# An FFN, RWKV and routing block in another order, with inverses from logarithm and exponential

## The chip, the cores and the metric

One core of a Trainium2 chip runs the whole program. The metric is the device time of one execution in microseconds. The core has five engines with a queue each: TensorE (PE), VectorE (DVE), ScalarE (ACT), GpSimd (POOL) and SyncE (SP). They meet only through semaphores that the program waits on and raises.

## The reference

Two layers over 8 x 256 tokens of 128 channels, all in float32. The change is in the three middle steps:

```python
x = x + attention(layernorm(x))
x = x + ffn(layernorm(x))              # silu(x Wg) * (x Wu), then Wd; hidden 384
x = x + rwkv(layernorm(x))             # time mix, K V R, a scan over time, sigmoid(R) * wkv, Wo
x = x + moe(layernorm(x))              # softmax over 8 experts, top 2, capacity 320

# rwkv, one step in time: a running maximum keeps the exponentials in range
p = max(pp, U + k);  e1 = exp(pp - p);  e2 = exp(U + k - p)
y = (e1 * aa + e2 * v) / (e1 * bb + e2)
p2 = max(pp + w, k); e1b = exp(pp + w - p2); e2b = exp(k - p2)
aa, bb, pp = e1b * aa + e2b * v, e1b * bb + e2b, p2
```

`layernorm` divides by the root of variance plus 1e-5. The routing gives each token its two best experts and its place in each expert's list, which is a count over all tokens before it.

## The kernel before

Three phases stand one after the other: `attention_phase`, `mid_phase` (FFN, RWKV and routing, the only one that the diff touches) and `moe_phase`. The residual `x_res` stays in SBUF.

`mid_phase` works in four chunks of 512 tokens (two sequences of 256). For a chunk, the FFN (suffix f) normalises on ScalarE (`normalize_f`), transposes on TensorE through the bank `xt`, copies back on ScalarE (`copy_f`), makes three gate and three up products of 512 columns (HB is 3), a silu each on ScalarE, their product `h` on VectorE (`hidden`), and `down`. VectorE adds the result to `x_res` and takes mean and variance. The RWKV part (w) normalises, transposes and copies in the same way; `project_k`, `project_v`, `project_r` are two products each (this token and the one before); `running_max` is a scan on VectorE along time, `subtract_max` one more product into the bank of k; `weigh` makes the four exponentials e1b, e2b, e1, e2 on ScalarE (four relus and four Exp); `states` runs the scans aa and bb; `total` makes numerator and denominator; `invert` is VectorE's reciprocal; `finish` multiplies by it and by the gate (sigmoid, on ScalarE); `output` is the product with Wo. The routing part (m) adds, normalises and transposes again, makes logits (`logit`), and on VectorE `shift` (subtract the largest), `choose` (softmax and the two best) and `place` (slot numbers, from TensorE's `count`). GpSimd then writes the chunk's rows to DRAM with eight indirect DMAs.

The order on each engine is written by hand. In slot s the FFN works on chunk s, the RWKV part on chunk s - 1 up to its reciprocal, and `finish`, output and routing on chunk s - 2; `slot_of` of each engine's block lists the calls. There are six slots. A table load (`ACT_TABLE_LOAD`) is put in by the compiler wherever ScalarE goes to a function of another table set; the program doesn't name it. The inverse deviation of the layer norms is made on VectorE: an integer guess and three Newton steps (`rsqrt`, L69 to L77). The banks in PSUM: xt, u, y, d, v, r and two for the gates; logits go to u, the counts and both sums to y.

Of the kernel before, what the change touches and what calls it, by code (L numbers as in the profile page):

```python
# [885 lines left out]
def mid_phase(nc, ffn, wkv, moe, state, x_res, ln_ffn, sem_of, load_next):  # L886
# [6 lines left out]
    with ExitStack() as ctx:  # L893
# [3 lines left out]
        def bank(name):  # L897
# [13 lines left out]
        silu = [sb(f"silu{i}", [P, CW]) for i in range(2)]  # L911
# [23 lines left out]
        ln = normal_tiles(lambda n, s: sb("ln_" + n, s), 2 * TPC)  # L935
        OF_W, OF_M = 0, TPC
# [30 lines left out]
        def _(pool):  # L967
            g = nc.gpsimd
            g.memset(pp[:, :, 0:1], MIN_P).then_inc(consts, 1)
            g.memset(aa[:, :, 0:1], 0.0).then_inc(consts, 1)  # L970
            g.memset(bb[:, :, 0:1], 0.0).then_inc(consts, 1)
# [19 lines left out]
        def _(pe):
# [6 lines left out]

            def transpose_f(c):
                pe.wait_ge(xf_ready, c + 1)  # L1000
                if c > 1:
                    pe.wait_ge(xwT_ready, c - 1)
                transpose(lambda a: xf[:, a, :], tf_done)

            def transpose_w(c):
                pe.wait_ge(xw_ready, c + 1)
                if c > 1:
                    pe.wait_ge(xmT_ready, c - 1)
                elif c < LAST:
                    pe.wait_ge(xfT_ready, c + 2)  # L1010
                transpose(lambda a: xw[:, a, :], tw_done)

            def transpose_m(c):
                pe.wait_ge(xm_ready, c + 1)
                pe.wait_ge(xfT_ready, min(c + 4, CHUNKS))
                if c:
                    pe.wait_ge(xwT_ready, min(c + 2, CHUNKS))
                    pe.wait_ge(xmT_ready, c)
                transpose(lambda a: rows[:, c * TPC + a, 0:P], tm_done)

            def gate_and_up(c, k):
# [674 lines left out]
```

## Time and profile before

| what | value |
|---|---|
| median of 3 runs | 540.08 us (539.99 to 543.14) |
| the profiled execution | 542.5 us, its span 540.5 us |
| mean granted TensorE clock | 0.835 |
| `attention_phase` | 0 to 275.7 us |
| `mid_phase` with its scatters | 275.7 to 460.1 us |
| `moe_phase` | 460.1 to 540.5 us |
| busy in 275.7 to 303.0 us | PE 16.3, DVE 9.6, ACT 9.8 us |
| busy in 303.0 to 329.4 us | PE 18.2, DVE 16.8, ACT 14.9 us |
| busy in 400.7 to 428.6 us | PE 10.8, DVE 21.0, ACT 10.2 us |
| busy in 428.6 to 449.4 us | PE 5.6, DVE 10.7, ACT 3.7 us |

The profile is one execution; the span runs from its first instruction to its last, and 2.0 us lie around it. Times in a timeline count from the span's start. A row gives start, duration, engine, line, operation, output and inputs, and in brackets the idle time before it and what ended it. The granted clock is the share of TensorE's full speed: 1.00 is its 2.4 GHz level, 0.50 its 1.2 GHz level.

### The profile page before, as it was taken

The numbers are of one execution on the slowest core, as the hardware profiler recorded it, in microseconds if no ns is written. First come the engines' busy times: TensorE is split into PE (matmuls) and PEld (weight loads), VectorE is DVE, ScalarE is ACT, GpSimd is POOL, SyncE is SP. The second block draws the span as 40 slices with busy tenths as digits, with TensorE's granted clock in tenths as the row PEclk, the third lists the DMA queues.
The fourth block names the chain that finished last, engine by engine and source line by source line (L and its number), as shares of the span: only waits on it lengthen the run. The fifth ranks groups of instructions, "written<-read, shape, count | busy, mean of one in ns | idle before, by whom it ended". The sixth has DMA issues, their size and how long they took to land. (4 is left out here: it accounts for less than half of the span.)

```text
span 540.5 us, 6922 instructions
## 1 busy us (share of the span) xinstructions
PE 366.8 (68%) x2345; PEld 230.8 (43%) x2345; DVE 289.9 (54%) x706; ACT 235.2 (44%) x399; POOL 179.4 (33%) x342
## 2 busy tenths in 40 slices
PE   2779889898989898787474949478455120489930
PEld 1335454646464655454352434344323110368820
DVE  5646767484848566542634266775777741022224
ACT  1757776374848384431033254653425120163400
POOL 2225473535352647542230000005023135005550
PEclk9879999899999899987778787867767555589985
DMA  9300000000000000000038000001000000413317
GB/s 175 96 1 2 0 2 1 1 0 2 1 1 1 2 0 2 1 1 0 0 68 327 0 0 1 1 1 45 0 11 28 8 9 4 111 57 114 118 38 232
DMA packets 32257, 19.80 MB, mean 37 GB/s; under 512 B 12146, under 2 KB 29955, under 8 KB 31840
## 3 DMA queue, kind: packets, MB, share of 16 engines
q1 hardware_dynamic: 26128, 14.92, 9.8%
q0 software_dynamic: 1920, 2.89, 1.7%
q10 hardware_dynamic: 4176, 1.57, 1.1%
q8 instruction: 18, 0.29, 0.2%
q14 instruction: 15, 0.12, 0.1%
HBM read 12.12 MB, written 8.29 MB: 38 GB/s over the span
## 5 line engine op out<-in xcount | busy, mean ns | idle before, releaser
L537 DVE TENSOR_TENSOR at_attn<-at_sim,at_attn 128x1024 f32<-128x1024 f32 x64 | 75.4, 1219 | 54.7 <-ACT at_attn L414 54.5
L414 ACT ACTIVATE at_attn<-at_sim 128x1024 f32<-128x1024 f32 x64 | 62.2, 1028 | 49.4 <-PE at_sim L234 49.1
L987 POOL DMA_INDIRECT mo_slots<-ro_rows,ro_put x32 | 31.8, 995 | 142.7 <-DVE ro_put L1390 134.2
L251 PE MATMUL at_av<-at_attn,at_v_raw 128*64 128x256 f32 x512 | 64.1, 394 | 11.8 <-DVE at_v_raw L528 11.8
L631 POOL TENSOR_TENSOR at_osq<-at_ob 128x512 f32<-128x512 f32 x32 | 35.9, 1127 | 48.3 <-ACT at_ob L422 47.7
L271 PE MATMUL at_misc<-at_w_out,at_ob 128*128 128x128 f32 x256 | 39.3, 327 | 17.9 <-DVE at_ob L542 17.9
L251 PEld LDWEIGHTS at_av<-at_attn,at_v_raw 128*64 128x64 f32 x512 | 34.5, 139 | 37.4 <-DVE at_v_raw L528 15.0
L271 PEld LDWEIGHTS at_misc<-at_w_out,at_ob 128*128 128x128 f32 x256 | 38.0, 240 | 19.9 <-issue 18.8
L234 PE MATMUL at_sim<-at_q,at_k 32*128 32x256 f32 x512 | 38.7, 401 | 4.0 <-DVE at_attn L537 2.2
L1504 POOL DMA_INDIRECT mo_answers<-mo_ye,mo_to x24 | 22.8, 951 | 41.7 <-DVE mo_ye L1604 36.8
L200 PE MATMUL at_misc<-at_w_v,at_xnT 128*128 128x512 f32 x64 | 34.7, 644 | 0.6 <-ACT at_sq_v L392 0.5
L234 PEld LDWEIGHTS at_sim<-at_q,at_k 32*128 32x128 f32 x512 | 24.0, 184 | 18.0 <-issue 9.3
L422 ACT COPY at_ob<-at_av 128x512 f32<-128x512 f32 x32 | 18.8, 587 | 19.0 <-PE at_av L251 19.0
L1567 ACT ACTIVATE mo_hT<-mo_h,mo_b 128x320 f32<-128x320 f32 x32 | 16.3, 528 | 20.2 <-PE mo_h L1524 20.1
L521 DVE TENSOR_REDUCE at_z<-at_sq_v 128x16 f32<-128x1024 f32 x16 | 19.5, 1218 | 10.1 <-ACT at_sq_v L392 10.1
L1524 PE MATMUL mo_h<-mo_xeT,mo_w 128*128 128x320 f32 (+1 forms) x64 | 22.0, 493 | 3.5 <-ACT mo_hT L1567 2.6
L1533 PE MATMUL mo_y<-mo_w,mo_hT 128*128 128x128 f32 (+1 forms) x192 | 24.4, 281 | 0.0
L391 ACT COPY at_v_raw<-at_misc 128x512 f32<-128x512 f32 x32 | 18.8, 587 | 12.1 <-PE at_misc L200 12.0
L1533 PEld LDWEIGHTS mo_y<-mo_w,mo_hT 128*128 128x128 f32 (+1 forms) x192 | 23.0, 178 | 2.5 <-issue 0.6
L1600 DVE TENSOR_TENSOR mo_ye<-mo_y,mo_b 128x128 f32<-128x128 f32 (+1 forms) x24 | 5.4, 281 | 32.7 <-PE mo_y L1533 23.9
L528 DVE TENSOR_TENSOR at_v_raw<-at_v_raw,at_key_factor 128x1024 f32<-128x1024 f32 x16 | 19.9, 1282 | 5.7 <-POOL at_key_factor L651 5.5
L996 PE MATMUL mi_xt<-ff_ident,ro_rows 128*128 128x128 f32 x16 | 4.5, 433 | 26.8 <-ACT ro_rows L1141 26.8
(208 smaller groups left out, 678.1 us busy)
## 6 DMA issues: line engine op xcount, KB each, us to landing
mo_w<-in_L_ffn_w SPq DMA_DIRECT2D x16, 256.0 KB, 2.9
mo_answers<-mo_zero SPq DMA_DIRECT2D x2, 1024.0 KB, 12.3
mo_got<-mo_answers SPq DMA_DIRECT2D x8, 256.0 KB, 4.7
mo_slots<-mo_empty SPq DMA_DIRECT2D x1, 1440.0 KB, 9.5
mo_xe<-mo_slots SPq DMA_DIRECT2D x5, 256.0 KB, 4.4
x_res<-in_L_attn_tokens SPq DMA_DIRECT2D x4, 256.0 KB, 3.3
out<-x_res ACTq DMA_DIRECT2D x4, 256.0 KB, 2.7
at_w_v<-in_L_attn_Wkv ACTq DMA_DIRECT2D x1, 512.0 KB, 5.7
```

The costliest lines, as they stand in the source:

```text
L200: mm(bank[:, :], xnT[b % 2][:, t * P:(t + 1) * P], w_v[:, half * 512:(half + 1) * 512], start=True, stop=True).then_inc(v_done, 1)
L234: last = mm(sim[h // 2][:, h % 2, j * T:(j + 1) * T], k[b % 2][n % 2][at, n // 2, j * P:(j + 1) * P], q[b % 2][at, n // 2, :], start=True, ...
L251: last = mm(av[e * DV:(e + 1) * DV, half * T:(half + 1) * T], v_raw[b % 2][:, j, h * DV:(h + 1) * DV], attn[(2 * Q + half) % 4][:, e, j, : ...
L271: last = mm(bank[:, t * P:(t + 1) * P], ob[b % 3][:, s, t * P:(t + 1) * P], w_out[:, s, :], start=s == 0, stop=s == PAIRS - 1)
L414: nc.scalar.activation(attn[n % 4][:, :, :, :].rearrange("p e j t -> p e (j t)"), sim[half][:, :, :], ACT.Relu).then_inc(relu_ready, 1)
L528: last = v.tensor_tensor(heads, heads, key_factor[b % 2][:, t, :].unsqueeze(2).to_broadcast([P, HEADS, DV]), ALU.mult)
L537: v.tensor_tensor(r, sim[half][:, :, :], r, ALU.mult).then_inc(attn_ready, 1)
L631: g.tensor_tensor(osq[b % 2][:, 2 * n:2 * n + 2, :], o, o, ALU.mult).then_inc(osq_ready, 1)
L987: g.indirect_dma_start(moe.slots, bass.IndirectOffsetOnAxis(put[k][:, t:t + 1], 0), rows[:, t, :], None, bounds_check=SLOTS - 1, oob_is_er ...
L1504: g.indirect_dma_start(answers, bass.IndirectOffsetOnAxis(to[0:r, 3 * e + n:3 * e + n + 1], 0), ye[e % 2][0:r, n, :], None, bounds_check=2 ...
L1524: mm(h_bank[k][:, 0:CAPACITY], w1[e.par][:, k * P:(k + 1) * P], xeT[:, bass.ds(e.count(CAPACITY), CAPACITY)], start=True, stop=True).then_ ...
L1533: done = mm(y_bank[e.par][0:r, n * P:(n + 1) * P], hT[e.par][:, k, at:at + r], w2[e.par][:, k, :], start=k == 0, stop=k == KB - 1)
```

## The change

Everything is in `mid_phase`.

- **Order.** `slot_of` becomes `period`, for c from -3 to 4: gates and silus of chunk c + 3, ups, `h` and `down` of chunk c + 2, normalising and projections of chunk c + 1, the mixing of chunk c with its inverse, `finish` and output, and the routing of chunk c - 1. There is one gate bank instead of two, three `silu` tiles instead of two, and separate banks for the FFN's and the output's sums (`yf`, `yw`); logits and counts go to `yw`, those of the last chunk to `v`.
- **Inverses.** The reciprocal of the denominator is exp(-ln(den)) on ScalarE, in place on `inv_den`, with one Newton step in `finish`: numerator and denominator are both multiplied by it, q = (den*inv - 2) * num*inv, and -1 in the last product. The inverse deviation is exp(-0.5 ln(var + eps)) (`seeds`) with one Newton step of three VectorE instructions. At the end of each period ScalarE makes an Exp of one column into `spare`.
- **Joint sums.** aa and bb lie in one tile `sums`; e2 and e2*v in one tile `here`; `total` and the first product of `finish` work on both halves at once (1024 columns).
- **Waits.** `normalize_f(0)` comes after the wait for six constants, one of which needs the decay. GpSimd waits for each of the two columns of slot numbers apart.

```diff
@@ banks
-        xt, u_bank, y_bank, d_bank, v_bank, r_bank = (bank(n) for n in ("xt", "u", "y", "d", "v", "r"))
-        g_bank = [bank(f"g{i}") for i in range(2)]
+        xt, g_bank, u_bank, d_bank, v_bank, r_bank, yf_bank, yw_bank = (
+            bank(n) for n in ("xt", "g", "u", "d", "v", "r", "yf", "yw"))
...
@@ TensorE
-            def slot_of(f, x, m):
...
+            def gate_of(c, k):
+                n = HB * c + k
+                pe.wait_ge(xfT_ready, c + 1)
+                if n:
+                    pe.wait_ge(silu_ready, n)
+                mm(g_bank[:, :], ffn.w_gu[:, 0, k * P:(k + 1) * P], xfT[c % 2][:, :], start=True, stop=True).then_inc(gate_done, 1)
...
+            def period(c):
+                gates, hidden, ahead, behind = chunk(c + 3), chunk(c + 2), chunk(c + 1), chunk(c - 1)
+                if chunk(c):
+                    subtract_max(c)
...
+                if behind:
+                    count(c - 1)
+                if gates:
+                    gate_of(c + 3, 1)
+                if hidden:
+                    down(c + 2)
+                if gates:
+                    gate_of(c + 3, 2)
+                if chunk(c) and c < LAST:
+                    output(c)
...
@@ ScalarE
+            def seeds(c):
+
+                first, end = OF_W if chunk(c + 1) else OF_M, OF_M + TPC if chunk(c - 1) else OF_M
+                act.wait_ge(var_ready, c + 2)
+                nc.scalar.activation(ln["var"][:, first:end], ln["mv"][:, first:end, 1], ACT.Ln, bias=eps[:, :]).then_inc(log_var, 1)
+                act.wait_ge(log_var, c + 2)
+                nc.scalar.activation(seed[:, first:end], ln["var"][:, first:end], ACT.Exp, scale=-0.5).then_inc(seed_ready, 1)
+
+            def invert(c):
+
+                act.wait_ge(totals, c + 1)
+                if c:
+                    act.wait_ge(scaled_ready, c)
+                nc.scalar.activation(full(inv_den), total_of[:, 1, :, :], ACT.Ln).then_inc(log_ready, 1)
+                act.wait_ge(log_ready, c + 1)
+                nc.scalar.activation(full(inv_den), full(inv_den), ACT.Exp, scale=-1.0).then_inc(inv_ready, 1)
...
+            def period(c):
+                gates, ahead, behind = chunk(c + 3), chunk(c + 1), chunk(c - 1)
+                if chunk(c):
+                    weigh(c)
+                if ahead or behind:
+                    seeds(c)
+                if ahead:
+                    normalize_w(c + 1)
+                if behind:
+                    normalize_m(c - 1)
+                if ahead:
+                    copy_w(c + 1)
+                if chunk(c):
+                    invert(c)
...
+                if ahead:
+                    gate(c + 1)
+                if gates or ahead:
+                    nc.scalar.activation(spare[:, :], eps[:, :], ACT.Exp)
...
@@ VectorE
+            def inverse_deviations(c):
+
+                first, end = OF_W if chunk(c + 1) else OF_M, OF_M + TPC if chunk(c - 1) else OF_M
+                var, rstd, a, y = ln["mv"][:, first:end, 1], ln["rstd"][:, first:end], ln["a"][:, first:end], seed[:, first:end]
+                dve.wait_ge(seed_ready, c + 2)
+                link(stt(a, var, LN_EPS, y, ALU.add, ALU.mult))
+                link(stt(a, a, -0.5, y, ALU.mult, ALU.mult))
+                link(stt(rstd, a, 1.5, y, ALU.add, ALU.mult))
+                shifts(ln["shift"], ln, first, end, ln_ready)
...
-                link.done(tt(full(t2), full(e2), by_batch(v_bank), ALU.mult))
+                tt(here[:, 0, :, :], e2, by_batch(v_bank), ALU.mult).then_inc(v_used, 1)
                 dve.wait_ge(sums_ready, 2 * c + 2)
-                link.done(tt(full(t3), full(e1), bb[:, :, 0:T], ALU.mult))
-                tt(full(t1), full(e1), aa[:, :, 0:T], ALU.mult).then_inc(v_used, 1)
-                link.wait()
-                tt(full(den), full(t3), full(e2), ALU.add).then_inc(den_ready, 1)
+                link(tt(past[:, :, :, :], sums[:, :, :, 0:T], e1[:, :, :].unsqueeze(1).to_broadcast([P, 2, NB, T]), ALU.mult))
                 dve.wait_ge(v_used, c + 1)
-                tt(full(num), full(t2), full(t1), ALU.add).then_inc(totals, 1)
...
+                tt(total_of[:, :, :, :], past[:, :, :, :], here[:, :, :, :], ALU.add).then_inc(totals, 1)
...
-                link(tt(full(num), full(num), full(inv_den), ALU.mult))
+                tt(scaled[:, :, :, :], total_of[:, :, :, :], inv_den[:, :, :].unsqueeze(1).to_broadcast([P, 2, NB, T]),
+                   ALU.mult).then_inc(scaled_ready, 1)
+                dve.wait_ge(scaled_ready, c + 1)
+                link(stt(full(q), scaled[:, 1, :, :], -2.0, scaled[:, 0, :, :], ALU.add, ALU.mult))
                 dve.wait_ge(gated, c + 1)
...
+                stt(full(rw), full(q), -1.0, by_batch(r_bank), ALU.mult, ALU.mult).then_inc(rw_ready, 1)
...
+            def period(c):
+                behind = chunk(c - 1) and c <= LAST
+                form = chunk(c + 2)
+                if c == 0:
+                    variances(c)
+                if chunk(c):
+                    running_max(c)
+                if c and (chunk(c + 1) or behind):
+                    variances(c)
+                if c == -1:
+                    hidden(c + 2, 0)
+                if chunk(c):
+                    states(c)
+                if chunk(c + 1) or behind:
+                    inverse_deviations(c)
+                if chunk(c):
+                    total(c)
+                if form and c != -1:
+                    hidden(c + 2, 0)
+                if chunk(c):
+                    finish(c)
+                if behind:
+                    shift(c - 1)
+                if c == LAST:
+                    variances(c + 1)
+                    inverse_deviations(c + 1)
...
```

On TensorE, from the start of `mid_phase` (mi_xt transposes, mi_g gates, mi_u ups, mi_y and mi_yf down, mi_d the projection k), before:

```order
L996 MATMUL mi_xt<-ff_ident,mi_xf 128x128 x4
L1026 MATMUL mi_g<-mi_xfT,ff_w_gu 128x512
L1031 MATMUL mi_u<-mi_xfT,ff_w_gu 128x512
L1026 MATMUL mi_g<-mi_xfT,ff_w_gu 128x512
L1031 MATMUL mi_u<-mi_xfT,ff_w_gu 128x512
L1026 MATMUL mi_g<-mi_xfT,ff_w_gu 128x512
L1031 MATMUL mi_u<-mi_xfT,ff_w_gu 128x512
L996 MATMUL mi_xt<-ff_ident,mi_xf 128x128 x4
L1041 MATMUL mi_y<-ff_w_dn,mi_h 128x128 x12
L996 MATMUL mi_xt<-ff_ident,mi_xw 128x128 x4
```

and in the changed program:

```order
L1013 MATMUL mi_xt<-ff_ident,mi_xf 128x128 x4
L1040 MATMUL mi_g<-mi_xfT,ff_w_gu 128x512 x3
L1047 MATMUL mi_u<-mi_xfT,ff_w_gu 128x512 x2
L1013 MATMUL mi_xt<-ff_ident,mi_xf 128x128 x4
L1047 MATMUL mi_u<-mi_xfT,ff_w_gu 128x512
L1040 MATMUL mi_g<-mi_xfT,ff_w_gu 128x512 x2
L1055 MATMUL mi_yf<-ff_w_dn,mi_h 128x128 x12
L1040 MATMUL mi_g<-mi_xfT,ff_w_gu 128x512
L1047 MATMUL mi_u<-mi_xfT,ff_w_gu 128x512
L1013 MATMUL mi_xt<-ff_ident,mi_xw 128x128 x4
```

The three gates of a chunk now stand ahead of its ups, and `down` of chunk 0 comes behind chunk 1's first two gates.

On ScalarE, from the end of `weigh` of chunk 1 (ro_rows and mi_xw are normalised rows of the routing and the RWKV part, mi_xmT and mi_xwT their transposed copies), before:

```order
L1200 ACTIVATE mi_e<-mi_u 128x512 x2
L1165 COPY mi_xfT<-mi_xt 128x512
L1141 ACTIVATE ro_rows<-x_res,mi_ln_shift,mi_ln_rstd 128x128 x4
L1177 COPY mi_xmT<-mi_xt 128x512
L1141 ACTIVATE mi_xw<-x_res,mi_ln_shift,mi_ln_rstd 128x128 x4
L1208 ACTIVATE mi_logits<-mi_logits 128x32
L1171 COPY mi_xwT<-mi_xt 128x2x256
```

and in the changed program:

```order
L1225 ACTIVATE mi_here<-mi_u 128x512
L1231 ACT_TABLE_LOAD
L1231 ACTIVATE mi_ln_var<-mi_ln_mv,mi_eps 128x8
L1233 ACT_TABLE_LOAD
L1233 ACTIVATE mi_seed<-mi_ln_var 128x8
L1166 ACTIVATE mi_xw<-x_res,mi_ln_shift,mi_ln_rstd 128x128 x4
L1166 ACTIVATE ro_rows<-x_res,mi_ln_shift,mi_ln_rstd 128x128 x4
L1196 COPY mi_xwT<-mi_xt 128x2x256
L1240 ACT_TABLE_LOAD
L1240 ACTIVATE mi_inv_den<-mi_total 128x512
L1242 ACT_TABLE_LOAD
L1242 ACTIVATE mi_inv_den<-mi_inv_den 128x512
```

Two logarithms and two exponentials have come in, with a table load ahead of each; the inversion stands behind both normalisings and `copy_w`.

On TensorE, the end of the phase (mi_rw the RWKV result, mi_mask the chosen experts), before:

```order
L1076 MATMUL mi_y<-wk_w_o,mi_rw 128x128 x4
L996 MATMUL mi_xt<-ff_ident,ro_rows 128x128 x4
L1086 MATMUL mi_u<-mo_rw,mi_xmT 128x8 x4
L1096 MATMUL mi_y<-mi_mask,mi_tri 128x32
L1100 MATMUL mi_y<-mi_mask,mi_ones 128x32 x12
```

and in the changed program:

```order
L1102 MATMUL mi_yw<-mo_rw,mi_xmT 128x8 x4
L1091 MATMUL mi_yf<-wk_w_o,mi_rw 128x128 x4
L1110 MATMUL mi_yw<-mi_mask,mi_tri 128x32
L1114 MATMUL mi_yw<-mi_mask,mi_ones 128x32 x8
L1114 MATMUL mi_yw<-mi_mask,mi_ones 128x24
L1114 MATMUL mi_yw<-mi_mask,mi_ones 128x16
L1114 MATMUL mi_yw<-mi_mask,mi_ones 128x8
L1013 MATMUL mi_xt<-ff_ident,ro_rows 128x128 x4
L1102 MATMUL mi_v<-mo_rw,mi_xmT 128x8 x4
```

Output 3 now stands ahead of the count of chunk 2, and the last chunk's transposes behind that count.

## Rows read from the trace of the kernel before

**Rows 1.** Stretches, two middle slots: us, busy of PE, PEld, DVE, ACT, POOL; clock

```profile
329.40:364.80 35.40, 24.50 (x86) 13.82 (x85) 25.01 (x78) 17.87 (x32) 0.00 (x0) 0.78 0.00 1
364.80:400.70 35.90, 22.04 (x78) 12.91 (x78) 24.96 (x79) 13.40 (x24) 7.95 (x8) 0.74 0.05 17
```

**Rows 2.** Waits, 275 to 461 us: total us, times, longest us

```profile
ACT mi_silu L1184 <- PE mi_g L1026: 29.8, 11, 7.2
```

**Rows 3.** Timeline of ScalarE, first relus of `weigh`: start us, us

```profile
310.64 1.24 ACT L1197 ACTIVATE mi_u<-mi_d,mi_decay 128x512 f32<-128x512 f32 x2
...
338.39 1.24 ACT L1197 ACTIVATE mi_u<-mi_d,mi_decay 128x512 f32<-128x512 f32 x2
...
374.25 1.26 ACT L1197 ACTIVATE mi_u<-mi_d,mi_decay 128x512 f32<-128x512 f32 x2
...
404.27 1.26 ACT L1197 ACTIVATE mi_u<-mi_d,mi_decay 128x512 f32<-128x512 f32 x2 [9.72 <-PE mi_d L1058]
```

**Rows 4.** Timelines of VectorE and GpSimd, the last `place` and the last scatter

```profile
447.55 0.19 DVE L1384 TENSOR_SCALAR mi_over<-mi_y 128x32 f32<-128x32 f32 x1 [0.68 <-PE mi_y L1100]
...
449.19 0.17 DVE L1390 CAST ro_put<-mi_top 128x4 uint32<-128x4 f32 x1
...
459.05 0.97 POOL L987 DMA_INDIRECT mo_slots<-ro_rows,ro_put  x1 [0.30 <-issue]
```

**Rows 5.** Timeline of ScalarE, `weigh` of chunk 0 and a small exponential

```profile
311.90 1.28 ACT L1200 ACT_TABLE_LOAD   x1
313.20 0.63 ACT L1200 ACTIVATE mi_e1b<-mi_u 128x512 f32<-128x512 f32 x1
...
315.39 1.14 ACT L1200 ACTIVATE mi_e<-mi_u 128x512 f32<-128x512 f32 x2
...
355.98 0.23 ACT L1208 ACTIVATE mi_logits<-mi_logits 128x32 f32<-128x32 f32 x1 [1.18 <-DVE mi_logits L1356]
```

**Rows 6.** Timeline of ScalarE, `normalize_w` and `copy_w` of chunk 1

```profile
322.05 1.65 ACT L1141 ACTIVATE mi_xw<-x_res,mi_ln_shift,mi_ln_rstd 128x128 f32<-128x128 f32 x4 [5.04 <-DVE mi_ln_shift L1247]
324.90 0.59 ACT L1171 COPY mi_xwT<-mi_xt 128x512 f32<-128x512 f32 x1 [1.21 <-PE mi_xt L996]
```

**Rows 7.** Timeline of VectorE: inverse deviation, sums, reciprocal, end of `choose`

```profile
293.02 0.17 DVE L1290 TENSOR_SCALAR mi_ln_var<-mi_ln_mv 128x4 f32<-128x4 f32 x1
...
295.41 0.16 DVE L1247 SCALAR_TENSOR_TENSOR mi_ln_shift<-mi_ln_mv,mi_ln_rstd 128x4 f32<-128x4 f32 x1
...
321.93 0.68 DVE L1323 TENSOR_TENSOR mi_t<-mi_e,mi_v 128x512 f32<-128x512 f32 x1
...
324.94 3.35 DVE L1334 RECIPROCAL mi_inv_den<-mi_den 128x512 f32<-128x512 f32 x1
...
359.55 0.18 DVE L1377 SCALAR_TENSOR_TENSOR ro_rows<-mi_hot,mo_tokens 128x32 f32<-128x32 f32 x1
```

**Rows 8.** Timeline of TensorE: down, transposes, projections, `subtract_max`

```profile
288.10 2.84 PE L1041 MATMUL mi_y<-ff_w_dn,mi_h 128*128 128x128 f32 x24
...
297.31 1.11 PE L996 MATMUL mi_xt<-ff_ident,mi_xw 128*128 128x128 f32 x4 [6.36 <-ACT mi_xw L1141]
299.19 2.05 PE L1046 MATMUL mi_d<-mi_xwT,wk_w_old_k 128*128 128x512 f32 x2 [0.77 <-ACT mi_xwT L1171]
301.03 1.91 PE L1047 MATMUL mi_d<-mi_xwT,wk_w_k 128*128 128x512 f32 x2
...
309.53 1.02 PE L1046 MATMUL mi_v<-mi_xwT,wk_w_old_v 128*128 128x512 f32 x2
...
366.28 2.08 PE L1058 MATMUL mi_d<-mi_pp,wk_minus 128*128 128x512 f32 x2 [3.13 <-DVE mi_pp L1302]
```

**Rows 9.** Stretches, columns as in rows 1: one low, one high clock

```profile
297.00:303.00 6.00, 4.93 (x9) 2.50 (x10) 0.02 (x1) 0.84 (x2) 0.00 (x0) 0.50 0.00 0
...
331.00:344.00 13.00, 12.73 (x57) 7.70 (x55) 6.81 (x17) 8.81 (x16) 0.00 (x0) 1.00 0.00 1
```

**Rows 10.** The page's part 5: a VectorE product of 1024 columns, in attention

```profile
L537 DVE TENSOR_TENSOR at_attn<-at_sim,at_attn 128x1024 f32<-128x1024 f32 x64 | 75.4, 1219 | 54.7 <-ACT at_attn L414 54.5
```

More of the change, by code:

```diff
@@ L910, in mid_phase @@
         xf, xfT = sb("xf", [P, TPC, P]), [sb(f"xfT{i}", [P, CW]) for i in range(2)]
-        silu = [sb(f"silu{i}", [P, CW]) for i in range(2)]
+        silu = [sb(f"silu{i}", [P, CW]) for i in range(HB)]
         h = sb("h", [P, HB, CW])
@@ L956, in mid_phase, with chunk @@
         block = ctx.enter_context(nc.Block())
-        def chunks(s):
-            return tuple(c if 0 <= c < CHUNKS else None for c in (s, s - 1, s - 2))
+        def chunk(c):
+            return 0 <= c < CHUNKS
+        PERIODS = range(-3, CHUNKS + 1)
         @block.sync
@@ L1131, in _ @@
             pe.wait_ge(ffn.w_ready, 2)
-            transpose_f(0)
-            for s in range(CHUNKS + 2):
-                slot_of(*chunks(s))
+            for c in PERIODS:
+                period(c)
         @block.scalar
@@ L1186, in weigh @@
             def weigh(c):
                 act.wait_ge(d_done, c + 1)
-                if c:
-                    act.wait_ge(sums_ready, 2 * c)
-                    act.wait_ge(totals, c)
-                for pair, exps in enumerate(((e1b, e2b), (e1, e2))):
-                    below, above = ((decay[:, 0:1], decay[:, 1:2]), (cols[:, 1:2], minus_u[:, :]))[pair]
+                for half, exps in enumerate(((full(e1b), full(e2b)), (full(e1), e2))):
+                    below, above = ((decay[:, 0:1], decay[:, 1:2]), (cols[:, 1:2], minus_u[:, :]))[half]
+                    if c and half:
+                        act.wait_ge(totals, c)
+                    elif c:
+                        act.wait_ge(sums_ready, 2 * c)
@@ L1278, in add_mixed, with variances @@
[L1278 to L1295 removed]
+            def variances(c):
+                f, m = c + 1, c - 1
+                if chunk(f):
+                    dve.wait_ge(down_done, f + 1)
+                    add(f, yf_bank, xf_added)
+                if chunk(m):
+                    dve.wait_ge(out_done, m + 1)
+                    add(m, out_bank(m), xw_added)
+                if chunk(f):
+                    dve.wait_ge(xf_added, f + 1)
+                    statistics(f, OF_W)
+                if chunk(m):
+                    dve.wait_ge(xw_added, m + 1)
+                    statistics(m, OF_M)
+                if chunk(f) and f:
+                    dve.wait_ge(xw_ready, f)
+                if chunk(m) and m:
+                    dve.wait_ge(xm_ready, m)
+                link.wait()
+                for a in range(OF_W if chunk(f) else OF_M, OF_M + TPC if chunk(m) else OF_M):
+                    last = v.bn_aggr(ln["mv"][:, a, :], ln["stats"][:, a, :])
+                last.then_inc(var_ready, 1)
@@ L1353, in shift @@
                 dve.wait_ge(logits_done, c + 1)
-                link(tt(full(logits), u_bank[:, 0:TPC * EXPERTS].rearrange("p (t e) -> p t e", e=EXPERTS), each(rb), ALU.add))
+                link(tt(full(logits), route_bank(c)[:, 0:N].rearrange("p (t e) -> p t e", e=EXPERTS), each(rb), ALU.add))
                 link(v.reduce_max(top[:, :], full(logits), AX.X))
@@ L1422, in _ @@
             dve.wait_ge(consts, 6)
-            for s in range(CHUNKS + 2):
-                slot_of(*chunks(s))
+            for c in range(-2, CHUNKS):
+                period(c)
+            shift(LAST)
+            choose(LAST)
+            place(LAST)
 def moe_phase(nc, inputs, state, a, out, x_res, sem_of):
```

282 lines of the change are left out of this document (109 added, 173 removed).

## The prediction

> **What bounds the kernel now.** I read the stretches of the profile first: what the change touches runs from 275.7 us to the last scatter's end at 460.0 [rows 4], 184.3 of the 540.5 us of the span, and no engine fills it. In the two middle slots (329.4 to 400.7 us) VectorE is busy 50.0 of 71.3 us, TensorE 46.5, ScalarE 31.3 [rows 1]. The waits say why: ScalarE alone waits 29.8 us for TensorE's gates, in 11 pieces [rows 2]; TensorE waits 6.4 us for ScalarE's normalised rows at 297.3 and 3.1 for VectorE's scan at 366.3 [rows 8]. It is a ring of three engines in which work passes from one to the next. So it is the length of one way round that counts, and the timeline gives it. I use as its beat the start of the first relu of `weigh`: 310.64, 338.39, 374.25 and 404.27 us [rows 3]. After the last there are 45.1 us to the end of the last `ro_put` cast (449.36) and 10.7 more to the end of the last scatter (460.02) [rows 4].
>
> **The prices** that I take. `weigh`: relus 1.26 us, table load 1.28, then 3.33 from the first exponential to the end of the last (313.20 to 316.53) [rows 5]; so 4.6 without the load. Four normalising activations 1.65 us, a copy of 128x512 0.6 [rows 6]. A chained VectorE step of 4 or 8 columns 0.2 us [rows 7]. The routing choice takes 3.45 us with its wait for the exponential (356.21 to 359.73) [rows 5, 7], `place` 1.8 (447.55 to 449.36) [rows 4]. TensorE: four transposes 1.1 us, or half of it, one product of 512 columns 1.9 us at a pitch of 1.84, or 1.0 [rows 8] (a projection is two: 3.7 or 1.9); the first price of each stands where the granted clock is 0.50 (the 1.2 GHz level), the second where it is 1.00 (2.4 GHz) [rows 9]. TensorE was at the low level after 6.4 and 3.1 us of idling [rows 8].
>
> **What is taken out.** VectorE loses the reciprocal of 3.35 us per chunk [rows 7], and 13 chained steps of the inverse deviation and shifts (293.02 to 295.57, 2.55 us) become 4 (0.8). Its five sums (321.93 to 324.94, a pitch of 0.60 [rows 7]) become one of 512 and two of 1024 columns: the nearest row of 1024 is 1.22 us [rows 10], so 3.0 again. `finish` has 1024, 512 and 512 columns instead of two of 512: 2.6 us for 1.4. The exponentials' load ahead of `weigh` moves to the end of the period, after the gate.
>
> **What is put in.** The trace has no Ln. I price it as the Exp rows of its two sizes, 0.23 us (128x32) and 0.63 (128x512) [rows 5]; an Ln of twice the price would add 0.8 us a period. What weighs more is the order of the change's program: it has a table load ahead of each Ln and one ahead of each Exp that follows it. Every load here takes 1.28 us [rows 5], so the seeds take 1.28 + 0.23 + 1.28 + 0.23 = 3.0 us between `weigh` and the shifts, and the inversion 1.28 + 0.6 + 1.28 + 0.6 = 3.8 us on ScalarE, behind `normalize_w`, `normalize_m` and `copy_w`, where VectorE's 3.35 us lay beside other engines' work and delayed only `place` and the next scan.
>
> The load rows are also where a page can be weighed. The exponential that follows the load starts at 313.20, 0.02 us after its end, and the relu before ended at 311.88, 0.02 us ahead of it [rows 3, 5]: a switch costs 1.3 us in this kernel. The Trainium skill ("ScalarE: Activation LUTs", What ACT_TABLE_LOAD costs) gives 1283 ns too, but adds a drain of 1380 ns, 2.66 us for each switch; with some 21 more switches on the path that would add an estimated 29 us. The trace shows no such drain, and the sum leaves it out.
>
> **The front.** Before, chunk 0 went through gate, up and down in one go, down ending at 290.94, and the first `weigh` began at 310.64 [rows 3, 8]. Now three periods stand ahead of period 0. I walk them with the prices above, from ScalarE's first normalising at 276.7 (some 0.7 us later than before, as it now waits for the decay too): normalised, transposed and copied at 279.75, gate 0 (1.4) ends 281.2; with one gate bank each gate waits for the silu before, so gate 2 ends 285.3; ups 0 and 1, transposes of chunk 1 (after a load of 1.3 and 1.65 of normalising) to 289.8, up 2, gates 1.0 and 1.1, and only then down 0: 293.2 to 296.1, against 290.9. ScalarE's silu of gate 1.2, the spare load, Ln and Exp with their loads put the seeds at 302.2, the normalised chunk at 304.75; transposes (1.1), copy and `project_k` (low level) to 310.4; up, chunk 2's transposes, `project_v`, up, `project_r`, two gates to 318.8; down 1 to 321.5. VectorE's order has chunk 1's variances ahead of the first scan, so scan 0 begins only at 323.7. ScalarE meanwhile: last silu 323.1, load and gate 325.0, load and spare Exp 326.5. First `weigh`: 326.5, which is 15.9 us later.
>
> **The periods,** each from `weigh` (0). Period 0: seeds 7.6, shifts 8.45, normalised 10.15, transposed 11.35, copied 12.0, inversion 15.8, normalising chunk 3 17.45, its transposes and copy 18.85; TensorE: `project_v` 20.0, up, `project_r` 22.6, gate, silu, gate 25.2, down 28.0, gate 28.9; silu 29.5, load and gate 31.4, load and spare 32.9. So 32.9 (before 27.75): 5.15 more. Period 1: shifts 8.45, two normalisings 11.7, copy 12.3, inversion 16.1, `finish` 18.8, `shift` 19.5, an `h` and the routing choice (3.45) 23.6, last `h` 24.3, `place` (1.8) 26.1 beside down 3 (27.2), output 28.1, `subtract_max` 29.1: 29.1 (before 35.86), 6.75 less. Period 2: the same to 18.8, `shift` 19.5, choice 23.3, count and `place` 25.8, scan 27.2, `subtract_max` 29.0 (before 30.02): 1.0 less. The last: one normalising ends 10.15, inversion 14.0, `finish` 16.7, output 3 at the low level 18.85, sum and variances 20.85, seeds 22.65, shifts 23.5; then VectorE does the choice of chunk 2 (27.0), count, `place` 29.4; TensorE's count 2 stands ahead of the transposes of chunk 3 (28.6), copy 29.25, logits 31.15, `shift`, choice 35.6, count, `place` 38.0 (before 45.1): 7.1 less. POOL's scatters come every 1.27 us (0.97 and 0.30 idle [rows 4]): chunk 2's eight run from 29.5 to 39.7, so chunk 3's end at 49.6 (before 55.75), which gives back 1 us.
>
> **Sum:** +15.9 + 5.15 - 6.75 - 1.0 - 6.15 = +7.1 us. The phase after it (80.4 us) is not changed. The profiled execution took 542.5 us, 2.0 around its span of 540.5; the sum makes it 549.6. It was 2.4 above the median of 540.1, so on the median: 547.2 us, 1.3% more.
>
> **Rivals.** *TensorE fast throughout* (24 in 100). The low level costs the walk 0.7 + 0.5 + 1.9 + 0.2 in the front, 0.5 in period 0, 0.6 in period 2 and 1.0 + 0.5 + 0.8 at the end, 6.7 us: 540.5, no change. Against it, waits of 3 us and more remain in every period, and such waits lowered the clock [rows 8, 9].
> *TensorE slow in the front* (18). The gates now pause 0.65 us for each silu, which the trace never shows in a row. If the clock stays at 1.2 GHz to the first scan, some ten products of 512 columns (0.85 each) and a down (2.84) cost 9 to 11 us more: 557 us.
> *VectorE is the bound after all* (10), the other side. Its work falls by 4 x (3.35 - 1.2) + 6 x 1.75 us, 19 in all; were it busy all round, that came off whole and the front's delay would vanish under it: 521 us. It is busy 70% in the middle slots [rows 1], so it decides only where it never waits; it waits for ScalarE's seeds and inverse by the new order.
> *No switch between Ln and Exp* (6), also faster. On the path are 2 loads in the front, 4 in each of periods 0 to 2 and 5 in the last: 19 x 1.28 = 24.3 us, 523 us; below 6 of them left, it is no slower than before. Against it: the order lists all of them. The Trainium skill ("ScalarE: Activation LUTs", Table sets: the hidden batching unit) has this rule, one load for ln and exp in a joint set; no run here shows it.
> The forecast itself has 42.
>
> **How the numbers follow.** The forecast's own range is 543 to 552: the Ln bound (+3), 2 to 4 us of the clock either way. The whole range is 537 to 558: up to the slow front, down past the fast clock; the two cases at 521 and 523 are left out with 16 in 100. A measurement tells about 1% from no change (534.7 to 545.5). Faster takes the cases of 521 and 523 but for 2 in 100, where half of what they take off is given back: 0.14. Same takes those 2, the fast clock's 24 and 4 of the forecast's low edge: 0.30. Slower is the rest: 0.56.
>
> **What would show it.** In the changed profile: the first `weigh` relu near 326 us (310 to 315 would break the front's step); beats of 33, 29 and 29 us after it; a load of 1.28 us before each Ln and each Exp of seeds and inverse, with nothing between but the Ln; the last cast near 455 us and the last scatter near 467, with its eight following chunk 2's without a pause. I am wrong if down 0 ends before 293, or if the inversion ends less than 3 us after `copy_w`.

## The result and the profile after

The changed kernel takes 551.55 us (median of 4 runs, 550.41 to 555.24) against 541.61 us for before beside it (4 runs): a ratio of 1.019, 95% interval 1.012 to 1.026. It is slower, by 9.9 us on the medians; 547.2 was forecast. The profiled execution took 550.4 us, its span 548.5. Busy time has moved from VectorE to ScalarE. The page's part 1 of after, busy time and share of the span:

```profile
PE 361.9 (66%) x2345; PEld 225.2 (41%) x2345; DVE 274.3 (50%) x642; ACT 272.3 (50%) x447; POOL 179.3 (33%) x342
```

Before had VectorE at 289.9 us and ScalarE at 235.2. The timeline of after, with the rows that answer to [rows 3, 4] and the start of the phase (start, duration, engine, line, operation, in brackets the wait):

```profile
274.00 1.65 ACT L1166 ACTIVATE mi_xf<-x_res,mi_shift_ffn,ln_rstd_of_ffn 128x128 f32<-128x128 f32 x4 [0.36 <-POOL mi_decay L992]
...
327.41 1.25 ACT L1222 ACTIVATE mi_u<-mi_d,mi_decay 128x512 f32<-128x512 f32 x2
...
359.92 1.25 ACT L1222 ACTIVATE mi_u<-mi_d,mi_decay 128x512 f32<-128x512 f32 x2
...
388.61 1.26 ACT L1222 ACTIVATE mi_u<-mi_d,mi_decay 128x512 f32<-128x512 f32 x2 [3.71 <-PE mi_d L1072]
...
417.77 1.26 ACT L1222 ACTIVATE mi_u<-mi_d,mi_decay 128x512 f32<-128x512 f32 x2 [5.88 <-PE mi_d L1072]
...
455.87 0.17 DVE L1433 CAST ro_put<-mi_top 128x4 uint32<-128x4 f32 x1
...
466.50 0.97 POOL L1004 DMA_INDIRECT mo_slots<-ro_rows,ro_put  x1 [0.30 <-issue]
```

The ruler of all that follows is cut from these rows: the front (first normalising of chunk 0 to the first `weigh` relu), three beats from `weigh` to `weigh`, the tail (last `weigh` to the end of the last scatter) and their sum, the phase. Unlike the total it leaves out when the phase begins, which varied between executions from 274.0 to 282.1 us though nothing ahead of it was edited.

| us | front | beats | tail | phase | ratio to before (95%) |
|---|---|---|---|---|---|
| before | 34.6 | 27.8, 35.9, 30.0 | 55.8 | 184.0 | |
| after | 53.4 | 32.5, 28.7, 29.2 | 49.7 | 193.5 | 1.019 (1.012 to 1.026) |
| g1: after, joint table set | 50.3 | 29.9, 27.5, 25.7 | 46.6 | 180.1 | 0.994 (0.990 to 0.999) |
| g2: new order alone | 53.9 | 31.5, 27.1, 26.0 | 50.3 | 188.8 | 1.007 (1.003 to 1.012) |
| h2: the same again | 53.9 | 31.5, 27.1, 26.0 | 48.5 | 187.0 | 1.003 (0.997 to 1.008) |
| g3: inverses alone, old order | 36.6 | 29.7, 33.8, 28.7 | 56.3 | 185.0 | 1.001 (0.997 to 1.005) |
| g4: g3 with the joint set | 36.1 | 27.1, 31.1, 25.1 | 52.8 | 172.3 | 0.982 (0.974 to 0.990) |
| h3: after, three gate banks | 50.0 | 32.5, 28.7, 29.2 | 49.7 | 190.1 | 1.012 (1.008 to 1.016) |
| h4: g1, chunk 0 straight through | 43.9 | 39.6, 27.6, 25.7 | 44.9 | 181.7 | 0.994 (0.989 to 1.000) |
| i1: joint set and gate banks | 46.9 | 29.9, 27.5, 25.6 | 44.9 | 174.8 | 0.979 (0.971 to 0.987) |
| i2: g4, reciprocal on VectorE | 38.7 | 25.9, 34.9, 27.5 | 53.2 | 180.1 | 0.979 (0.968 to 0.990) |

Ratios and intervals leave out executions over 1.5% above the fastest of the same kernel, so that they can differ from the quotient of two medians, and the profiles of g2 and h2 are of such executions, though their fronts and beats agree with each other to 0.1 us.

After against before: +18.8 in the front, +4.8, -7.2 and -0.8 in the beats, -6.1 in the tail, +9.5 us in the phase. A phase difference of 5.4 us is 1% of the time, and by that most ratios fit their phases to about 0.4% (i2 is the exception, see there).

### The profile page after: what moved, and what is told of

It reads as the page before. It is cut to its first block and busy times, and to the rows that moved or that the text cites. A ratio compares the mean times of both kernels' runs of the same rounds, so it can differ in the third digit from the quotient of the medians.

```text
span 548.5 us, 6912 instructions
## 1 busy us (share of the span) xinstructions
PE 361.9 (66%) x2345; PEld 225.2 (41%) x2345; DVE 274.3 (50%) x642; ACT 272.3 (50%) x447; POOL 179.3 (33%) x342
## 5 line engine op out<-in xcount | busy, mean ns | idle before, releaser
L251 PEld LDWEIGHTS at_av<-at_attn,at_v_raw 128*64 128x64 f32 x512 | 34.6, 139 | 37.1 <-DVE at_v_raw L528 14.8
L271 PE MATMUL at_misc<-at_w_out,at_ob 128*128 128x128 f32 x256 | 37.7, 318 | 17.9 <-DVE at_ob L542 17.9
L271 PEld LDWEIGHTS at_misc<-at_w_out,at_ob 128*128 128x128 f32 x256 | 36.4, 231 | 19.9 <-issue 18.8
L200 PE MATMUL at_misc<-at_w_v,at_xnT 128*128 128x512 f32 x64 | 33.8, 628 | 0.7 <-ACT at_sq_v L392 0.6
L1013 PE MATMUL mi_xt<-ff_ident,mi_xw 128*128 128x128 f32 x16 | 4.5, 435 | 38.2 <-ACT mi_xw L1166 38.2
L422 ACT COPY at_ob<-at_av 128x512 f32<-128x512 f32 x32 | 18.8, 587 | 18.2 <-PE at_av L251 18.2
L1622 ACT ACTIVATE mo_hT<-mo_h,mo_b 128x320 f32<-128x320 f32 x32 | 16.3, 529 | 20.6 <-PE mo_h L1579 20.5
L391 ACT COPY at_v_raw<-at_misc 128x512 f32<-128x512 f32 x32 | 18.8, 587 | 11.2 <-PE at_misc L200 11.1
## 6 DMA issues: line engine op xcount, KB each, us to landing
mo_slots<-mo_empty SPq DMA_DIRECT2D x1, 1440.0 KB, 10.4
```

Source lines behind the costliest of these rows:

```text
L200: mm(bank[:, :], xnT[b % 2][:, t * P:(t + 1) * P], w_v[:, half * 512:(half + 1) * 512], start=True, stop=True).then_inc(v_done, 1)
L251: last = mm(av[e * DV:(e + 1) * DV, half * T:(half + 1) * T], v_raw[b % 2][:, j, h * DV:(h + 1) * DV], attn[(2 * Q + half) % 4][:, e, j, : ...
L271: last = mm(bank[:, t * P:(t + 1) * P], ob[b % 3][:, s, t * P:(t + 1) * P], w_out[:, s, :], start=s == 0, stop=s == PAIRS - 1)
```

## The experiments

Runs that share a first letter were made together, each with its own runs of before. The medians of before were 544.95 (g), 542.15 (h) and 544.83 us (i), which is why ratios and phases are compared and not medians.

**g1: the loads between logarithm and exponential.** After, but the one-column Exp at the end of a period is replaced by a load of the table set that holds both functions; the compiler then needs no load ahead of Ln and Exp, and 14 of 34 loads of the phase are left (the expectation below takes 28 for the 34; the 20 that fall away are right).

```diff
-                    nc.scalar.activation(spare[:, :], eps[:, :], ACT.Exp)
+                    nc.scalar.preload_act_table_set("natural_log_exp_and_others")
```

> The changed kernel with one edit: at the end of a period ScalarE loads the table set that has both Ln and Exp, instead of making an Exp of one column, so that no load stands between Ln and Exp (20 of 28 loads in this phase fall away, 8 of them the inversion's, 12 the seeds'). Theory (the switches are on the path): 2.8 us less in the front, some 4 in each of periods 0 to 2 and 6 at the end, about 21 in all: 528 to 532 us, faster than the kernel before. Rival (the loads lie beside other engines' work, the front's delay is the whole loss): 546 us or more.

Measured: 541.92 us, ratio 0.994; the phase is 13.4 us shorter than after's. After's ScalarE in period 0, from its timeline:

```profile
331.90 1.28 ACT L1231 ACT_TABLE_LOAD   x1
333.19 0.30 ACT L1231 ACTIVATE mi_ln_var<-mi_ln_mv,mi_eps 128x4 f32<-128x4 f32 x1
333.51 1.28 ACT L1233 ACT_TABLE_LOAD   x1
334.80 0.21 ACT L1233 ACTIVATE mi_seed<-mi_ln_var 128x4 f32<-128x4 f32 x1
...
338.68 0.59 ACT L1196 COPY mi_xwT<-mi_xt 128x512 f32<-128x512 f32 x1 [1.21 <-PE mi_xt L1013]
339.29 1.28 ACT L1240 ACT_TABLE_LOAD   x1
340.58 0.63 ACT L1240 ACTIVATE mi_inv_den<-mi_total 128x512 f32<-128x512 f32 x1
341.23 1.28 ACT L1242 ACT_TABLE_LOAD   x1
342.52 0.63 ACT L1242 ACTIVATE mi_inv_den<-mi_inv_den 128x512 f32<-128x512 f32 x1
```

And g1's in period 1:

```profile
362.68 0.31 ACT L1231 ACTIVATE mi_ln_var<-mi_ln_mv,mi_eps 128x8 f32<-128x8 f32 x1
363.02 0.21 ACT L1233 ACTIVATE mi_seed<-mi_ln_var 128x8 f32<-128x8 f32 x1
364.49 1.65 ACT L1166 ACTIVATE mi_xw<-x_res,mi_ln_shift,mi_ln_rstd 128x128 f32<-128x128 f32 x4 [1.26 <-DVE mi_ln_shift L1294]
...
368.06 0.63 ACT L1240 ACTIVATE mi_inv_den<-mi_total 128x512 f32<-128x512 f32 x1
368.71 0.63 ACT L1242 ACTIVATE mi_inv_den<-mi_inv_den 128x512 f32<-128x512 f32 x1
...
375.09 0.23 ACT L1250 ACTIVATE mi_logits<-mi_logits 128x32 f32<-128x32 f32 x1 [5.08 <-DVE mi_logits L1401]
```

There is no load between the two functions: the loads are real time, and the gain has the sign of the theory but about two thirds of its 21 us. Period 1 shows where the rest went. From `weigh` to the end of the inverse g1 takes 11.0 us and after 16.0 (359.92 to 375.90), 5.0 less. At the exponential of the logits 2.5 us are left of it (16.8 against 19.3), at the next `weigh` 1.2 (27.5 against 28.7). The wait of 5.08 us in the last row is for VectorE, and VectorE waits for TensorE's logits. Their rows in g1:

```profile
368.30 1.09 PE L1013 MATMUL mi_xt<-ff_ident,ro_rows 128*128 128x128 f32 x4 [0.99 <-ACT mi_xwT L1196]
369.18 1.92 PE L1060 MATMUL mi_d<-mi_xwT,wk_w_old_k 128*128 128x512 f32 x2
370.89 1.92 PE L1061 MATMUL mi_d<-mi_xwT,wk_w_k 128*128 128x512 f32 x2
372.59 1.72 PE L1102 MATMUL mi_yw<-mo_rw,mi_xmT 128*128 128x8 f32 x8
374.16 2.05 PE L1047 MATMUL mi_u<-mi_xfT,ff_w_gu 128*128 128x512 f32 x2
...
371.36 0.69 DVE L1390 SCALAR_TENSOR_TENSOR mi_rw<-mi_q,mi_r 128x512 f32<-128x512 f32 x1
374.42 0.19 DVE L1399 TENSOR_TENSOR mi_logits<-mi_yw,mo_rb 128x32 f32<-128x32 f32 x1 [2.37 <-PE mi_yw L1102]
```

and in after:

```profile
376.48 1.04 PE L1102 MATMUL mi_yw<-mo_rw,mi_xmT 128*128 128x8 f32 x8
...
377.93 0.69 DVE L1390 SCALAR_TENSOR_TENSOR mi_rw<-mi_q,mi_r 128x512 f32<-128x512 f32 x1
...
379.19 0.23 ACT L1250 ACTIVATE mi_logits<-mi_logits 128x32 f32<-128x32 f32 x1 [2.82 <-DVE mi_logits L1401]
```

In g1 `project_k` stands ahead of `logit` and both run at the low level (the granted clock is 0.50 from 368.3 to 374.3), so the logits come at 374.3, 2.3 us behind `finish` (371.36 + 0.69); in after they were ready when `finish` ended (logits 376.48 + 1.04, `finish` 378.6).

The end of g1 also holds a late start: VectorE's first `place` instruction begins 3.9 us after its forerunner, where i1 and after show 0.7. The row in g1:

```profile
446.28 0.19 DVE L1427 TENSOR_SCALAR mi_over<-mi_v 128x32 f32<-128x32 f32 x1 [3.88 <-remote]
```

What it waited for isn't known. 1.7 us of it reach the last scatter. Without them the loads are worth 15.1 us of phase, and between h3 and i1 below, where neither has a late start, they are worth 15.3.

**g2 and h2: the order alone.** New order, banks and joint sums, but the inverses on VectorE as before (`rsqrt` and one reciprocal per chunk).

```diff
-                link(stt(a, var, LN_EPS, y, ALU.add, ALU.mult))
-                link(stt(a, a, -0.5, y, ALU.mult, ALU.mult))
-                link(stt(rstd, a, 1.5, y, ALU.add, ALU.mult))
+                link(v.tensor_scalar(var, ln["mv"][:, first:end, 1], LN_EPS, None, ALU.add))
+                rsqrt(nc, link, rstd, var, a, rstd.bitcast(I32), var.bitcast(I32))
...
+                v.reciprocal(full(inv_den), total_of[:, 1, :, :]).then_inc(inv_ready, 1)
```

> The changed kernel's order, banks and joint sums, but with VectorE's inverses of the kernel before (reciprocal right behind the sums, rsqrt with three Newton steps; no seeds and no inversion on ScalarE). Theory (the order gains in the mixing periods about what its front costs, the switches are the loss): front some 15 us later than before, beats some 2 us shorter than in the changed kernel: 540 to 545 us, as before. Rival A (the order is what pays, once the switches are gone): 530 us or less. Rival B (the order itself is the loss): 549 us or more.

> The order of the change with the inverses of before, once more, for a second profile and interval. In the first profile the front (first normalising of chunk 0 to the first weigh relu) took 53.9 us, the beats after it 31.5, 27.1, 26.0 and 50.3 us to the last scatter's end. Theory (the low TensorE clock of the gates and ups of chunk 0 belongs to the order, since each gate waits for the silu before): the front is again 52.5 to 54.5 us, and the time 0.4 to 1.2% above before. Rival (it belonged to that execution): the front is 49.5 to 51 us with the ups of chunk 0 near 1.0 us each, and the time within 0.3% of before.

Measured: 549.09 and 546.12 us, ratios 1.007 and 1.003. The order with its banks and joint sums (no run takes these apart) gains nothing; it costs 3.0 us of phase in h2 and 4.8 in g2, which has a late start as g1 has, though one of the two intervals takes in no change. g2 lies between its theory and rival B: the 549 us of the rival are reached, but beside a before of 544.95. h2's front is as its theory has it, its time only 0.3% above before. The front is 53.9 us both times: what the order adds there (19.3 us) is more than the three beats and the tail give back (14.5 to 16.3).

**g3: the inverses alone.** Before's order, with Ln and Exp on ScalarE for both inverses and a load ahead of each.

```diff
+                if f is not None or m is not None:
+                    seeds(s, f, m)
                 if m is not None:
                     normalize_m(m)
...
                 if x is not None:
+                    invert(x)
                     gate(x)
```

> The order of the kernel before, with the change's inverses alone: seeds and inversion by Ln and Exp on ScalarE (a load ahead of each), one Newton step each, no reciprocal and no three-step rsqrt on VectorE; the inversion stands behind copy_w, where ScalarE idles. Theory (ScalarE has idle time there in the old order, so most loads are hidden and VectorE's 3.35 us ahead of place and the next scan come off): 2 us less in each of four slots, 532 to 537 us. Rival (the inverses lose wherever they stand): 545 us or more.

Measured: 543.95 us, ratio 1.001, phase 185.0: no change, and neither the theory's 532 to 537 us nor the rival's 545, though VectorE lost its 3.35 us per chunk (and took two more products in `finish`). The second beat gains 2.1 and the third 1.3; the front loses 2.0, the first beat 1.9, the tail 0.5.

**g4: the same with the joint set.**

```diff
                     for k in range(HB):
                         silu_of(f, k)
+                nc.scalar.preload_act_table_set("natural_log_exp_and_others")
```

> As the one before (old order, inverses by Ln and Exp), with the set that has both Ln and Exp loaded once a slot behind the silus. Theory: the load between the Ln and the Exp of the seeds, 1.28 us, is on the path in five slots, and the loads ahead of weigh go too: 6 us less than with the switches, 526 to 531 us, the fastest of the four. Rival (loads all hidden in the old order): the same as with the switches within 2 us.

Measured: 531.78 us, ratio 0.982, phase 172.3, 12.7 us under g3's and so twice the 6 us of the theory. It beats both kernels. In the second slot the inverse costs ScalarE 1.3 us and no load:

```profile
356.82 0.63 ACT L1216 ACTIVATE mi_inv_den<-mi_den 128x512 f32<-128x512 f32 x1
357.49 0.63 ACT L1218 ACTIVATE mi_inv_den<-mi_inv_den 128x512 f32<-128x512 f32 x1
```

So the switches are worth about the same in either order (15.1 to 15.3 us in the new one, 12.7 in the old), and with them gone the old order leads the new one by 7.8 (by 6.1 without g1's late start).

The two halves of the change don't simply add. By phase the order costs 3.0 us (h2) and the inverses 1.0 (g3), together 9.5. In the new order the switches cost some 2.5 us more, and without them ScalarE's inverses gain less: 8.7 us (h2 to g1 without its late start) against 11.7 (before to g4).

**h3: the low clock in the front.** After, with the gates of chunk 0 in three banks that are still free there.

```diff
+        def gate_bank(c, k):
+            return (g_bank, yw_bank, r_bank)[k] if c == 0 else g_bank
...
-                if n:
+                if c:
                     pe.wait_ge(silu_ready, n)
```

> The changed kernel, but the three gates of chunk 0 go to three banks that are still free there (g, yw, r), so that none waits for the silu before. Theory (the front grew from the walked 49.8 to 53.4 us because the pauses between gates hold TensorE at its 1.2 GHz level): gates end near 281.5 instead of 284.2, the ups of chunk 0 run at 1.0 to 1.4 us instead of 1.9 to 2.05, the front takes 49 to 50.5 us, and the time is 3 to 4 us (0.6 to 0.8%) under the changed kernel's: 1.010 to 1.014 of before. Rival (the front hangs on ScalarE's and VectorE's chain behind down 0, which has slack before it): down 0 starts earlier, but the front stays within 1 us of 53.4 and the ratio at 1.017 to 1.020.

Measured: 549.11 us, ratio 1.012; front 50.0, and every beat and the tail within 0.1 us of after's. TensorE in after (the pieces of a product of 512 columns):

```profile
279.58 2.04 PE L1040 MATMUL mi_g<-mi_xfT,ff_w_gu 128*128 128x512 f32 x2 [0.78 <-ACT mi_silu L1208]
282.40 2.05 PE L1040 MATMUL mi_g<-mi_xfT,ff_w_gu 128*128 128x512 f32 x2 [0.78 <-ACT mi_silu L1208]
284.24 1.91 PE L1047 MATMUL mi_u<-mi_xfT,ff_w_gu 128*128 128x512 f32 x2
287.12 2.04 PE L1047 MATMUL mi_u<-mi_xfT,ff_w_gu 128*128 128x512 f32 x2 [0.97 <-DVE mi_h L1302]
...
290.11 1.62 PE L1047 MATMUL mi_u<-mi_xfT,ff_w_gu 128*128 128x512 f32 x2
291.57 1.02 PE L1040 MATMUL mi_g<-mi_xfT,ff_w_gu 128*128 128x512 f32 x2
```

and in h3:

```profile
281.67 1.92 PE L1043 MATMUL mi_yw<-mi_xfT,ff_w_gu 128*128 128x512 f32 x2
283.37 1.46 PE L1043 MATMUL mi_r<-mi_xfT,ff_w_gu 128*128 128x512 f32 x2
284.66 1.02 PE L1050 MATMUL mi_u<-mi_xfT,ff_w_gu 128*128 128x512 f32 x2
286.65 1.10 PE L1050 MATMUL mi_u<-mi_xfT,ff_w_gu 128*128 128x512 f32 x2 [0.97 <-DVE mi_h L1305]
```

After stays at 1.2 GHz for 14.5 us (277.10 to 291.57, granted clock 0.53, then 1.00); h3 leaves it after 4.4 (280.29 to 284.66, granted clock 0.61, then 1.00). The two pauses of 0.78 us that the silus make between the gates are what the edit takes out, 1.6 us in all, and it brings 3.4 us on the front. Taken off h2's phase of 187.0 that leaves the new order level with before's 184.0; this is an estimate, no run shows it.

**h4: chunk 0 straight through.** g1, but down 0 and 1 ahead of the next gates, and chunk 0's scan, `subtract_max` and `weigh` ahead of chunk 2's silus.

```diff
+                if c == -1:
+                    subtract_max(0)
+                if c in (-2, -1):
+                    down(c + 2)
                 if gates:
                     gate_of(c + 3, 0)
...
+                if c == -1:
+                    weigh(0)
                 if gates:
                     for k in range(HB):
                         silu_of(c + 3, k)
```

> The new order with the joint table set (first run of that: 0.994 of before, front 50.3 us), but chunk 0 goes straight through: down 0 and down 1 stand ahead of the next chunk's gates, and the first scan, subtract_max and weigh ahead of chunk 2's silus. Theory (of the 15.7 us by which the new front is longer, most is the work of chunks 1 and 2 put ahead of chunk 0): the first weigh begins 38 to 42 us after the first normalising instead of 50.3, the first beat grows from 29.9 to 34 to 36 us by the silus and gates it now holds, and the time falls by 4 to 8 us, to 0.980 to 0.987 of before. Rival (the work is only moved, the total of front and first beat counts): front and first beat together stay within 1.5 us of 80.2, and the ratio is 0.991 to 0.997.

Measured: 542.44 us, ratio 0.994, as g1. The front falls by 6.4 to 43.9, the first beat grows by 9.7 to 39.6: together 83.5 where g1 has 80.3. The theory falls. The rival has the ratio right, but the two stretches together are 3.3 us longer, more than its 1.5: the work of chunks 1 and 2 is not only moved, it costs a little more there, and why isn't known. (The rest of the phase is 1.6 us shorter, which is g1's late start at its end.)

**i1: both repairs.** h3's banks and g1's load together; the edits are those two.

> The changed kernel with both repairs: the joint table set (alone 0.994 of before, 180.1 us from the first normalising to the last scatter's end) and three banks for the gates of chunk 0 (alone 1.012, 190.1 us against 193.5). Theory (the two costs lie one behind the other in the front and add up): front 46.5 to 47.5 us, the phase 176 to 177.5 us, ratio 0.985 to 0.990. Rival (without the loads ScalarE isn't on the front's path, or the later low clock takes it back): front above 49, ratio 0.992 to 0.997.

Measured: 534.82 us, ratio 0.979; front 46.9, phase 174.8. They add up: 3.5 us off g1's front, 3.4 off after's. (The phase is 1.2 us under the theory's range, whose g1 had the late start in it.) It beats before and after. Its phase is 2.5 us above g4's; by the ratios, 0.979 and 0.982, the two can't be told apart.

**i2: which inverse pays.** g4, with the reciprocal back on VectorE.

```diff
-                    invert(x)
                     gate(x)
...
+                v.reciprocal(full(inv_den), full(den)).then_inc(inv_ready, 1)
```

> The old order with the joint table set again, but only the inverse deviations come from ScalarE; the reciprocal of the denominator stays on VectorE, one of 3.35 us per chunk as before. With both on ScalarE the phase took 172.3 us and the ratio was 0.982. Theory (the reciprocal stands ahead of place and the next scan on VectorE, so most of the 11.7 us come from its move, 2 to 2.5 us in each of four chunks): the phase takes 179 to 182 us, ratio 0.992 to 0.997. Rival (the inverse deviations, each on the path of the beat, are what pays): the phase stays under 175 us, ratio 0.981 to 0.987.

Measured: phase 180.1, as the theory has it, but ratio 0.979 (0.968 to 0.990), lower than the phase says and too wide to tell; the medians, 537.59 and 544.83 us, give 0.987. By the profiles the move of the reciprocal brings 7.8 of g4's 11.7 us. Its row ahead of `place` in the slot where g4 has none:

```profile
360.04 3.35 DVE L1355 RECIPROCAL mi_inv_den<-mi_den 128x512 f32<-128x512 f32 x1
```

By the ratios the question stays open.

## Why the prediction came out as it did

**The sign and the ring: right.** The work comes in periods that pass round the engines; 16 us less work for VectorE made nothing faster. The phase in one row, before and then after (us, busy time of PE, PEld, DVE, ACT, POOL; clock):

```profile
276.04:460.02 183.98, 97.41 (x352) 56.62 (x352) 107.83 (x357) 69.91 (x125) 37.20 (x40) 0.71 0.11 37
```

```profile
274.00:467.47 193.47, 94.56 (x352) 52.55 (x352) 91.84 (x292) 106.74 (x172) 36.85 (x39) 0.72 0.11 35
```

Most of the sum was confirmed row by row. Walked and measured: first `weigh` 326.5 and 327.4; beats 32.9, 29.1, 29.0 and 32.5, 28.7, 29.2; last `weigh` to the last cast 38.0 and 38.3, to the end of the last scatter 49.6 and 49.7, with chunk 3's eight scatters behind chunk 2's without a pause, as foretold. Of the two signs of being wrong neither came: down 0 ended at 297.1, not before 293, and the inversion 3.9 us behind `copy_w`.

**The front: mis-sized by 3.6 us, and this is the whole miss.** The first `weigh` seemed to be off by 0.9 us only because the phase began at 274.0 in after's execution and not at 276.7. The front itself was walked at 49.8 us and took 53.4. The step that failed is the price of the gates and ups of chunk 0: "gate 2 ends 285.3", with 1.4 us for gate 0 and the high level soon after. From the phase's start that is 8.6 us and was 10.4 (284.4), and up 1 ended 15.2 us after the start, where it took 10.6 in h3. At the end of down 0 the whole miss is there:

```profile
294.30 2.84 PE L1055 MATMUL mi_yf<-ff_w_dn,mi_h 128*128 128x128 f32 x24
```

That end is 23.1 us after the start, walked 19.4; from there to the first `weigh` it is 30.3, walked 30.4. That h3's front of 50.0 is 0.2 from the walk is partly luck: the walk kept the pauses and took the high clock, h3 has no pauses, reaches the end of down 0 0.9 us before the walk (18.5) and takes 1.1 us more from there. With 3.6 on top, the sum of +7.1 would have been +10.7, and the medians show +9.9. The 551.55 us are 4.4 above the forecast, at the upper end of its 543 to 552; 1.5 of this is before itself, 541.61 here and 540.08 there. The rival of a slow front had this mechanism, but took it to last until the first scan; it ended at 291.6, so it cost a third of the 9 to 11 us it was given. Small slips of the working: the choice's rows span 3.52 us and not 3.45, and 21 more switches stand beside the 19 of the rival; neither moves the sum by more than 0.2 us.

**ScalarE's prices: right.** An Ln takes 0.30 us at 128x4 and 0.63 at 128x512, where the Exp rows took 0.21 and 0.63, so the bound of twice the price wasn't needed. The inversion ended 3.9 us after `copy_w` (339.27 to 343.15, 3.8 forecast). The instruction that follows a load starts 0.01 to 0.05 us after it unless it waits for another engine, the one before ends 0.02 us ahead of it, and no drain is to be seen at any of the 34 loads; the page that the Trainium skill has on it ("ScalarE: Activation LUTs", What ACT_TABLE_LOAD costs) is right on the load and not on the drain for this kernel.

**VectorE's wait: named, not priced.** The forecast had the inverse behind two normalisings and a copy on ScalarE. After's waits, 327 to 456 us (total, times, longest):

```profile
DVE mi_scaled L1383 <- ACT mi_inv_den L1242: 15.1, 4, 4.6
...
DVE mi_ln_a L1342 <- ACT mi_seed L1233: 10.5, 5, 2.2
```

VectorE has 16.0 us less work and waits 25.6 us for what ScalarE now makes. Not all of that wait is on the path, so the two numbers don't balance, but they show why a lighter engine made nothing faster here.

**The rivals.** *TensorE fast throughout* fell: the granted clock is 0.72 over the phase, 0.71 before. *VectorE the bound* fell: in after VectorE is busy 91.8 of 193.5 us, 16.0 less than before and not the 19 of the rival, and the phase grew. g3 shows it for the old order, where 3.35 us a chunk came off it and the phase stayed. *No switch between Ln and Exp* did not happen, and g1 and g4 make it happen. Its 24.3 us were 19 loads laid end to end; the real gain of g1 is 13.4 (15.1 without its late start), since the next wait (the scans ahead of the shifts, `project_k` ahead of the logits) stands behind each. The rule of the Trainium skill ("ScalarE: Activation LUTs", Table sets: the hidden batching unit) that one set serves both ln and exp agrees with g1's rows, but only where the program loads that set itself: in after the compiler put a load ahead of each.

## What to carry to other kernels

Before moving a function to ScalarE, read in the order of instructions how many table loads it brings and whether one set holds all that follow each other; in this kernel the same arithmetic was worth +0.1% or -1.8% by that alone. An order that works ahead lengthens the front by all that it puts there, so set front, beats and tail side by side: a shorter beat is a gain only if there are enough of them. And a bank shared by three products can cost more than its waits (here 3.4 us for waits of 1.6), since TensorE can stay at its low clock meanwhile.

## What the runs showed of the hardware

- TensorE was at 1.2 GHz through 14.5 us of products of 2 us with three pauses of 0.78 to 0.97 between them, and left it after 4.4 us where the same products stood close together (after and h3; granted clock 0.53 and 0.61).
- It was also at 1.2 GHz in g1 for 9.2 us without any pause (368.30 to 377.5, granted clock 0.51), where after's TensorE rose after 4.3 us of the same work (372.17 to 376.48, granted clock 0.50). What makes the difference isn't settled.
- One VectorE instruction began 3.2 us (g1) and 3.1 us (g2) later than its inputs explain, in the same place in both and not in after, h2, h3, h4 and i1. Why isn't known.
- The table load took 1.283 us for each of the sets here, the joint one too.
